# One AND for the first masks of two steps, in a graph attention kernel on one core

## The reference

```python
A_tilde = A + jnp.eye(n, dtype=A.dtype)
mask = A_tilde > 0
Wh = (H @ W.T).reshape(n, HEADS, D_K)
e = score_l[:, :, None] + score_r.T[None, :, :]
e = jnp.where(e >= 0, e, NEG_SLOPE * e)
e = jnp.where(mask[:, None, :], e, -jnp.inf)
alpha = jax.nn.softmax(e, axis=2)
out = jnp.einsum('nhm,mhd->nhd', alpha, Wh).reshape(n, OUT_DIM)
x = _layernorm(x + jax.nn.elu(out), axis=-1)
```

## Time and profile before

| what | value |
|---|---|
| median of 3 runs | 1857.82 us (1857.31 to 1859.79) |
| profiled execution, its own time | 1858.71 us |
| span of the profile | 1856.8 us |
| mean granted TensorE clock | 0.969 of full speed |
| VectorE ANDs (L561) | 512 of 1219 ns, 624.1 us |
| VectorE XORs (L567) | 512 of 1218 ns, 623.8 us |
| VectorE compares (L549) | 598 of 747 ns, 439.7 us |
| ScalarE compares (L393) | 1450 of 1151 ns, 1545.5 us busy |
| TensorE mask products (L316) | 829.6 and 832.2 us |

### The profile page before, as it was taken

The page is one execution under the profiler, slowest core; times in us unless marked ns, Lnnn a source line. Parts: engine busy times, 40 slices in busy tenths (PEclk is TensorE's granted clock), DMA queues, the critical chain, the costliest instruction groups (busy, mean ns, idle before and its releaser), DMA issues.

```text
span 1856.8 us, 81511 instructions
## 1 busy us (share of the span) xinstructions
PE 1655.9 (89%) x37063; PEld 1622.3 (87%) x37063; DVE 1789.7 (96%) x2120; ACT 1723.1 (93%) x1855; POOL 42.5 (2%) x26
## 2 busy tenths in 40 slices
PE   6088899899999989899998999999998999989895
PEld 5088899798998989899997989989898989989895
DVE  5689999999999999999999999999999999999997
ACT  4599899899998999999998999999999999989994
POOL 1000000100000000010001000010000100010000
PEclk8598999999999999999999999999999999999998
DMA  6989777686766767676776867667777767666221
GB/s 218 352 291 347 242 228 257 212 266 224 246 207 222 260 218 244 218 248 218 233 240 214 267 217 249 212 234 245 229 233 234 251 200 263 216 219 209 58 73 35
DMA packets 240408, 420.05 MB, mean 226 GB/s; under 512 B 14400, under 2 KB 104896, under 8 KB 238016
## 3 DMA queue, kind: packets, MB, share of 16 engines
q1 hardware_dynamic: 240064, 414.83, 68.2%
HBM read 397.48 MB, written 17.30 MB: 223 GB/s over the span
## 4 chain that ended last, share of the span: by engine, by line
issue 80%; PE 5%; DMA 5%; ACT 4%; DVE 4%; POOL 2%; SPq 1%; POOLq 0%; DVEq 0%; ACTq 0%
ACT bmask L393 3%; DMA abuf<-in_adj_dram 3%; PE psum L316 3%; POOL vrs L711 1%; PE psum L270 1%; DMA v_scratch<-vt 1%; DVE bmask L561 1%; DMA vring<-v_scratch 1%; DVE bmask L549 1%; DVE cmask L567 0%; PE psum L279 0%; POOL vrs L708 0%; PE trp L303 0%; DVE acc L573 0%; DVE vt L503 0%
## 5 line engine op out<-in xcount | busy, mean ns | idle before, releaser
L393 ACT ACTIVATE bmask<-lrow,rtab 128x1024 fp8e4<-128x1024 f32 x1450 | 1545.5, 1151 | 45.3 <-PE psum L316 44.5
L316 PE MATMUL psum<-vring,bmask 128*128 128x99 bf16 x16384 | 829.6, 208 | 95.5 <-DVE bmask L561 46.5
L316 PEld LDWEIGHTS psum<-vring,bmask 128*128 128x128 fp8e4 x16384 | 765.8, 98 | 111.7 <-issue 81.3
L316 PE MATMUL psum<-vring,cmask 128*128 128x99 bf16 x16384 | 832.2, 209 | 24.3 <-DVE cmask L567 16.7
L316 PEld LDWEIGHTS psum<-vring,cmask 128*128 128x128 fp8e4 x16384 | 765.2, 98 | 35.9 <-DVE cmask L567 27.9
L561 DVE TENSOR_TENSOR bmask<-bmask,acache 128x1024 int32<-128x1024 int32 x512 | 624.1, 1219 | 12.3 <-ACT bmask L393 9.1
L567 DVE TENSOR_TENSOR cmask<-acache,bmask 128x1024 int32<-128x1024 int32 x512 | 623.8, 1218 | 11.0 <-PE psum L316 11.0
L549 DVE TENSOR_SCALAR bmask<-lrow,rtab 128x1024 fp8e4<-128x1024 f32 x598 | 439.7, 747 | 0.0
L303 PE MATMUL trp<-pack,abuf 128*128 128x32 bf16 x4096 | 143.4, 177 | 49.3 <-ACT acache L361 35.1
L303 PEld LDWEIGHTS trp<-pack,abuf 128*128 128x128 bf16 x4096 | 127.0, 97 | 53.8 <-issue 19.9
L361 ACT CAST acache<-trp 128x512 int32<-128x512 f32 x256 | 148.2, 579 | 12.3 <-PE trp L303 12.3
(11 more groups left out here) (59 smaller groups left out, 201.8 us busy)
## 6 DMA issues: line engine op xcount, KB each, us to landing
abuf<-in_adj_dram SPq DMA_DIRECT2D x256, 1024.0 KB, 8.1
vring<-v_scratch SPq DMA_DIRECT2D x512, 198.0 KB, 3.7
lrow<-l_scratch SPq DMA_DIRECT2D x16, 1024.0 KB, 11.0
v_scratch<-vt SPq DMA_DIRECT2D x16, 792.0 KB, 10.2
bmask<-in_x_dram SPq DMA_DIRECT2D x16, 256.0 KB, 3.0
late<-in_x_dram SPq DMA_DIRECT2D x32, 128.0 KB, 5.1
out_dram<-late SPq DMA_DIRECT2D x32, 128.0 KB, 6.4
l_scratch<-cmask SPq DMA_DIRECT2D x1, 128.0 KB, 3.7
```

The lines of the kernel that those rows point to most:

```text
L316: return nc.tensor.matmul(psum[:, bank, at * S3:(at + 1) * S3], mask[:, i, j * P:(j + 1) * P], vring[:, q % 4, i, col:col + S3], start=ope ...
L393: last = nc.scalar.activation(bmask[:, q % 4, h, i], lrow[:, p, h], ACT.Relu, bias=rtab[:, t, H + hh:H + hh + 1], scale=BIG, saturate=False)
```

## The change

mask_b is called for even q only and ANDs the masks of q and q + 1 in one instruction of 2048 words, with the four adjacency tiles of the two steps, each pair of tiles repeated for the two heads. It waits for the compares of q + 1 of both engines and for the adjacency tiles of q + 1. b_ready is raised once for two steps, and TensorE and mask_c wait for q // 2 + 1. VectorE's own compares move from one step ahead to two; compare(1) is made before the loop. ScalarE's compares, their count, the number of buffers and every other order stay.

```diff
--- before.py
+++ after.py
@@ -317,7 +317,7 @@
                                             vring[:, q % 4, i, col:col + S3], start=opening, stop=True, skip_group_check=True)
 
                 pe.wait_ge(v_in[q % 4], 16 * (q // 4 + 1))
-                pe.wait_ge(b_ready, q + 1)
+                pe.wait_ge(b_ready, q // 2 + 1)
                 for i in range(2):
                     for h in range(HP):
                         for j in range(SUB):
@@ -551,18 +551,21 @@
                 last.then_inc(cmp_dve, 1)
 
             def mask_b(q):
-                c, p, s = WHERE[q]
-                dve.wait_ge(evac_done, STEPS * c + s + 1)
-                dve.wait_ge(cmp_act, q + 1)
-                dve.wait_ge(cmp_dve, q + 1)
-                if s >= 4 * c or p > 0:
-                    dve.wait_ge(diag_done, 2 * c + (2 if p > 0 or s >= 4 * c + 2 else 1))
-                m = mask_words(bmask[:, q % 4])
-                nc.vector.tensor_tensor(m, m, adj_words(c, s), ALU.bitwise_and).then_inc(b_ready, 1)
+
+                c, p, s = WHERE[q]
+                dve.wait_ge(evac_done, STEPS * c + s + 2)
+                dve.wait_ge(cmp_act, q + 2)
+                dve.wait_ge(cmp_dve, q + 2)
+                if s + 1 >= 4 * c or p > 0:
+                    dve.wait_ge(diag_done, 2 * c + (2 if p > 0 or s + 1 >= 4 * c + 2 else 1))
+                m = words(bmask[:, q % 4:q % 4 + 2].rearrange("p k h i n -> p k h (i n)"))
+                at = (c * NT + 2 * s) % RING
+                four = words(acache[:, at:at + 4].rearrange("p t n -> p (t n)")).rearrange("p (k o n) -> p k o n", k=2, o=1)
+                nc.vector.tensor_tensor(m, m, four.to_broadcast([P, 2, HP, 2 * CI // 4]), ALU.bitwise_and).then_inc(b_ready, 1)
 
             def mask_c(q):
                 c, p, s = WHERE[q]
-                dve.wait_ge(b_ready, q + 1)
+                dve.wait_ge(b_ready, q // 2 + 1)
                 wait(dve, mm_done, q - 1)
                 nc.vector.tensor_tensor(mask_words(cmask[:, q % 2]), adj_words(c, s), mask_words(bmask[:, q % 4]),
                                         ALU.bitwise_xor).then_inc(c_ready, 1)
@@ -644,12 +647,14 @@
             add_diagonal(0, 0)
             add_diagonal(0, 1)
             compare(0)
+            compare(1)
             for q in range(Q):
                 c, p, s = WHERE[q]
                 w = c * NP + p
-                mask_b(q)
-                if q + 1 < Q:
-                    compare(q + 1)
+                if q % 2 == 0:
+                    mask_b(q)
+                if q + 2 < Q:
+                    compare(q + 2)
                 if s == 0 and w > 0:
                     take_first_sums(w - 1)
                 mask_c(q)
```

## The result

The changed kernel takes **1947.4 us** (median of 4 runs, 1944.28 to 1954.35) where the kernel before took 1858.8 beside it: ratio 1.048, 95% interval 1.0445 to 1.0514. The profiled execution took 1944.28 us, span 1942.5, against 1858.71 before: 85.6 us more.

A forecast was written before the change was run, and what follows sets the result against it. ScalarE was taken as slower inside a pass, VectorE as busiest through its turn work. Losses of 2.8 (pass 0), 5.0, 56 (passes 2 to 13), 4.5 and 2.5 made 71 us: 1858.7 + 71 = 1930 us, range 1888 to 1962.

The forecast's parts named there:

- several tens: Sign of being right: VectorE's idle time ahead of the joint AND, ended by ScalarE, grows from 9 us to this.
- (1) The joint AND's price: One AND of 2048 words takes 2289 ns, 2.21 us to the next start against 2.27; 17 us saved in all.
- (2) One step more of lead: Joint AND waits for ScalarE's compares of q+1, one step (3.1 us) more lead; 2.8 us late at step 224.
- (3) The later release: First products released 2.29 us after the AND's start instead of 1.22, XOR q 1.07 us later, ScalarE's buffer later.
- (4) The compares two steps ahead: VectorE's own compares wait for a free buffer in place of the XOR behind them; priced at nothing.
- The steady loss: Inside a pass, ScalarE waits for a mask buffer: 0.35 to 0.4 us lost in six steps.
- The turns: At an odd pass's turn ScalarE, without lead, stands 1.2, 1.05, 0.85, 1.1 and 0.8 us, sum 5.0.
- +5.0: Growth in us of an odd pass, from its turn at step 224: 109.1 where it now takes 104.1.
- +4.2 to 4.5: Growth in us of an even pass, from its turn at step 192; ScalarE reaches step 225 some 4.2 late.
- TensorE also slows: Rival, chance 0.17: longer gaps bring slower product groups, at a lower clock, to all 16 turns, adding 25 us: 1955.
- only the lead is lost: Rival, chance 0.18: buffers come as early as now, so each of 15 turns costs 2.8 us once: 1897.
- Faster: Rival, chance 0.07: ScalarE keeps more than 3.1 us of lead at every joint AND; VectorE's 17 us come off: 1841.

## Why the prediction was right

The forecast was 1930, the range 1888 to 1962; 1947.4 lies inside, and the sign and the mechanism are those that the runs show. Of the signs it named, VectorE's waits ahead of the joint AND came out larger than the "several tens", 114.3 us, and ScalarE's for products doubled; VectorE's share fell to 92%, and only 4.3 us of waits stand ahead of its compares. Step by step:

- **(1) The joint AND's price.** 2289 ns and 2.21 us to the next start, as forecast. Its saving never became time: with four buffers it is lost in VectorE's waits for ScalarE, with six in its waits for TensorE. The grouping rule of the Trainium skill (Perfetto Trace Analysis, Optimizing Scalar/DVE Operations) has the size of the saving right, 60 ns for the 65 of 2 x 1.14 against 2.21, but it asks for a saturated engine; 96% busy was not yet that. The other rule of that section of the Trainium skill, on splitting, fits the two runs with split ANDs only in part: splitting alone gave nothing that can be measured (1945.4 for 1947.4), splitting with separate waits 43 us.
- **(2) One step more of lead.** Right, and shown from both sides: taken from the kernel before it costs 47 us, given to the changed kernel (two steps) it returns everything. The run whose ANDs have their own waits, where the wait for q + 1 stands ahead of the XOR with one AND behind it, costs nearly as much as the first, 43.
- **(3) The later release.** Half right. XOR q behind more of the AND after the wait: 43 us, the difference of the two runs with two ANDs (1945.4 and 1902.5). The first products' later release, named in the same sentence: nothing behind the joint wait, by the run that released them early. The run with own waits also lets the first products of q go before the wait, so the 43 us aren't strictly the XOR's; but TensorE's waits for first products are nearly the same in the two runs (22.7 and 20.4 us), those for the second ones aren't (98.9 and 72.5). The direct try, the XOR ahead of the compares, gained nothing, at a cost of its own.
- **(4) The compares two steps ahead.** Nothing, as priced: 0.999.
- **The steady loss.** 0.5 us in six steps, of which 0.40 shows as idle; forecast 0.35 to 0.4. The forecast's own terms, 25.25 and 0.04 against 24.8, are nearer to 0.5. Its handoff of 0.15 from ScalarE to the joint AND was 0.09.
- **The turns.** At the turn to pass 7 the five stops were forecast as 1.2, 1.05, 0.85, 1.1 and 0.8, and were 1.19, 0.86, 0.68, 1.10 and 0.76. With the sixth of 0.73 and three steady ones of 0.40, 0.40 and 0.32 the pass has 6.4 us of idle time, as forecast (5.0 + 4 x 0.35).

**The terms that were mis-sized** are those of both kinds of pass, "+5.0" and "+4.2 to 4.5". The forecast counts a pass from its first AND to the next pass's. In the changed kernel these stand, for passes 6, 7 and 8 (to be laid beside 756.23, 867.70 and 971.78 in the earlier trace rows), at

```profile
784.65 2.28 DVE L564 TENSOR_TENSOR bmask<-bmask,acache 128x2048 int32<-128x2048 int32 x1
...
901.56 2.29 DVE L564 TENSOR_TENSOR bmask<-bmask,acache 128x2048 int32<-128x2048 int32 x1 [0.61 <-ACT bmask L393]
...
1011.83 2.29 DVE L564 TENSOR_TENSOR bmask<-bmask,acache 128x2048 int32<-128x2048 int32 x1 [0.83 <-ACT bmask L393]
```

Pass 6 grew by 5.4 us (111.5 to 116.9), pass 7 by 6.2 (104.1 to 110.3). On average the seven even passes from 2 to 14 grew by 5.6 where some 4.4 was forecast, the seven odd ones from 1 to 13 by 5.9 where it was 5.0. That is 8.4 + 6.1 = 14.5 of the 14.6 us between the 71 forecast and the 85.6 measured. (Counted from weigh_sums to weigh_sums, two steps later, the same loss divides into 5.9 and 5.5.) That pass 0 and the end of the kernel came out right together is luck: 1.0 us for 2.8, and 4.3 for 2.5.

In pass 7 the stops are as forecast, and ScalarE's work is not: it is busy 103.8 us there, where 102.7 was put (which is 102.5 by its own terms, 32 x 19.1/6 + 0.6). It was busy 103.1 before, and each of the nine stops takes away an overlap of some 0.1 us between two of its instructions. In pass 6 a part has another cause. TensorE's products there, ScalarE's next stop, and the engine totals of the stretch (the number behind the bracketed counts is the granted clock):

```profile
822.20 1.59 PE L316 MATMUL psum<-vring,bmask 128*128 128x99 bf16 x32 [2.84 <-DVE bmask L564]
...
850.80 1.83 PE L316 MATMUL psum<-vring,bmask 128*128 128x99 bf16 x32 [1.97 <-DVE bmask L564]
852.43 0.63 PE L303 MATMUL trp<-pack,abuf 128*128 128x32 bf16 x16
853.17 2.61 PE L316 MATMUL psum<-vring,cmask 128*128 128x99 bf16 x32
```

```profile
855.82 6.35 ACT L393 ACTIVATE bmask<-lrow,rtab 128x1024 fp8e4<-128x1024 f32 x6 [1.40 <-PE psum L316]
```

```profile
850.00:860.00 10.00, 9.10 (x180) 9.02 (x181) 10.00 (x11) 8.60 (x10) 0.00 (x0) 0.83 0.96 307
```

The joint AND waited for ScalarE, TensorE stood 1.97 us behind it, and then ran at a granted clock of 0.83 over the stretch, between its upper level of 2.4 GHz and the lower of 1.2. The 32 second products took 2.61 us instead of 1.60, and ScalarE stood 1.40 us for their buffer where 0.4 was worked out. That is the rival "TensorE also slows", at one place, on top of the forecast's mechanism. From 400 us on the changed kernel has 14 product groups of over 2.2 us (the first at 595.22, the last at 1819.63), the kernel before 6 (442.28 to 1521.24). How many of them lie on the path, and so how much of the 14.5 us is the clock's, stays open: no run changes the clock alone, and the traces don't settle it. Of the seven even passes the one that grew most, pass 12 by 7.8 us, has three of the 14, the one that grew least, pass 4 by 4.9, has two.

Of the other rivals, "only the lead is lost" is what the run with three buffers measures, 1905 where 1897 was worked out for it; the change lost that and nearly as much again. "Faster" needed 3.1 us of lead at every joint AND. With six buffers ScalarE had it, and VectorE's 17 us still did not come off, since VectorE then waited for TensorE, which that rival left out.

## What to carry to other kernels

Before merging instructions on the busiest engine, read how early its inputs are ready where they are latest, not on average: here a lead of 7 us had shrunk to 0.4 by the end of pass 6 (and to 1.6 or less at 14 of the 15 turns), and a merged instruction that asks for one step more paid for it in every pass, 89 us net of the 17 it saves. When a joint wait can't be avoided, put the work that is already possible ahead of it (half the loss came back that way), or add buffers first, and check which engine is next before counting the saving. What beats both is six mask buffers, with either form of the AND: 1850.6 and 1851.7 us, 0.5% faster than the kernel before.

## What was not expected of the hardware

On VectorE an instruction directly behind the one that it waits for started 0.1 to 0.3 us later than an independent one: 0.96 against 0.66 us behind a compare, 2.32 against 2.21 behind a joint AND, and 1.25 against 1.14 behind a single AND (the last AND and XOR of the kernel before, at 1831.49 and 1832.74). In the run with the XOR first that is 0.41 us a pair; if none of it were hidden, 256 pairs would make 105 us, more than the change itself cost. In the changed kernel one unrelated instruction between the two hides it. And TensorE's granted clock doesn't follow the length of a gap alone: behind the 2.84 us at 822.20 the 32 products took 1.59 us, with a granted clock of 1.00 in 820 to 830, behind the 1.97 us at 850.80 they took 1.83 and then 2.61, with 0.83 in 850 to 860.
